# Mixer's division: a reciprocal-root seed on ScalarE and a third-order step on VectorE and GpSimd in place of VectorE's reciprocal, with the stages around it reordered

## The reference, cut to what matters

```python
h = layernorm(x) * (1 + ca) + sa
r  = sigmoid(h @ W_r.T + b_r)
ek = exp(h @ W_k.T + b_k)
v  = h @ W_v.T + b_v
td, g = exp(b_td), exp(global_decay)
# over the 1024 steps of each sequence:
sa  = ek_t * v_t + td * sa
sb  = ek_t + td * sb
wkv = (g * ek_t * v_t + sa) / (g * ek_t + sb + 1e-6)
mem = 0.3 * mem + r_t * wkv - 0.05 * (mem > 0.05)
spk = mem > 0.05
# then
x = x + ga * spk
```

## Time and profile before

| | us |
|---|---|
| median of 3 runs | 558.91 (558.04 to 559.72) |
| profiled execution, first to last instruction (span) | 556.3 |
| busy: PE 488.8, VectorE 432.2, ScalarE 348.2, GpSimd 334.6 | |
| mixer up to the first membrane instruction | 0 to 46.55 |
| membrane passes | 46.55 to 81.9 |
| norm and first tiles of attention | 81.9 to 112 |
| steady attention, MLPs, LRU, experts | 112 to 556.3 |

### The profile page before, as it was taken

The page is one execution under the profiler, slowest core; times in us unless marked ns, Lnnn a source line. Parts: engine busy times, 40 slices in busy tenths (PEclk is TensorE's granted clock), DMA queues, the critical chain, the costliest instruction groups (busy, mean ns, idle before and its releaser), DMA issues.

```text
span 556.3 us, 11701 instructions
## 1 busy us (share of the span) xinstructions
PE 488.8 (88%) x4017; PEld 307.6 (55%) x4017; DVE 432.2 (78%) x1172; ACT 348.2 (63%) x1002; POOL 334.6 (60%) x259
## 2 busy tenths in 40 slices
PE   5650048999999999999989999999999999999997
PEld 3320014467777777543457777777644445667775
DVE  6999999889999886556899999985545688366665
ACT  4971004689999997532579999998647526533332
POOL 5860006999999997776889999995010277420000
PEclk9885559999999999999989999999999999999999
DMA  8400002311111112000041111111000000000000
GB/s 290 165 0 1 1 1 78 69 37 41 39 37 33 39 41 86 2 1 0 2 113 41 40 35 35 41 39 39 1 3 0 0 1 1 1 0 20 20 20 20
DMA packets 14880, 19.93 MB, mean 36 GB/s; under 512 B 2362, under 2 KB 8996, under 8 KB 14692
## 3 DMA queue, kind: packets, MB, share of 16 engines
q1 hardware_dynamic: 14532, 19.08, 12.7%
q10 hardware_dynamic: 288, 0.08, 0.1%
HBM read 8.94 MB, written 1.05 MB: 18 GB/s over the span
## 4 chain that ended last, share of the span: by engine, by line
PE 68%; DVE 14%; POOL 6%; ACT 6%; issue 4%; DMA 1%; DVEq 0%; POOLq 0%; ACTq 0%
PE psT L1396 11%; PE psQK L1469 9%; PE psO L1591 6%; PE psO L1523 5%; PE psQK L1798 5%; PE psS L1571 5%; DVE vst L990 3%; DVE vAB L994 3%; PE psO L1396 3%; PE psS L1870 3%; PE psQK L1605 3%; PE psS L1707 3%; PE psO L1870 2%; PE psQK L1730 2%; PE psO L1709 2%
## 5 line engine op out<-in xcount | busy, mean ns | idle before, releaser
L526 ACT ACTIVATE prob<-psS,nmx 128x128 f32<-128x128 f32 x256 | 89.9, 377 | 18.0 <-DVE nmx L1135 18.0
L819 POOL TENSOR_TENSOR rn<-ssq,half 128x16 f32<-128x16 f32 x32 | 93.0, 2907 | 8.0 <-DVE ssq L1121 7.9
L811 POOL TENSOR_TENSOR ra<-ra,rb 128x512 f32<-128x512 f32 x64 | 80.9, 1284 | 1.0 <-DVE rb L1103 0.9
L666 POOL TENSOR_TENSOR rst<-mv,half 128x4 f32<-128x4 f32 x24 | 25.7, 1070 | 73.8 <-DVE mv L922 63.6
L1469 PE MATMUL psQK<-wqkv,hsA 128*128 128x512 f32 x128 | 62.0, 604 | 1.0 <-DVE hsA L1084 0.6
L526 ACT ACTIVATION_READ_ACCUMULATOR prob<-psS,nmx 128x1 f32 x256 | 55.6, 217 | 0.0
L1100 DVE TENSOR_TENSOR ra<-psQK,rope 128x512 f32<-128x512 f32 x64 | 43.9, 686 | 10.2 <-PE psQK L1469 9.7
L827 POOL TENSOR_TENSOR qkn<-ra,rn 128x512 f32<-128x512 f32 x32 | 49.0, 1532 | 2.5
L1103 DVE TENSOR_TENSOR rb<-psQK,rope 128x512 f32<-128x512 f32 x64 | 43.6, 681 | 0.0
L647 ACT ACTIVATE gel<-psQK 128x512 f32<-128x512 f32 x32 | 19.1, 597 | 37.5 <-PE psQK L1798 37.5
L1114 DVE TENSOR_REDUCE ssq<-sq 128x8 f32<-128x512 f32 x64 | 41.1, 677 | 1.6 <-ACT sq L466 1.3
(11 more groups left out here) (240 smaller groups left out, 1204.1 us busy)
## 6 DMA issues: line engine op xcount, KB each, us to landing
vAB<-vAB SPq DMA_DIRECT2D x62, 128.0 KB, 2.2
wqkv<-in_wqkv SPq DMA_DIRECT2D x2, 768.0 KB, 8.4
big<-in_x SPq DMA_DIRECT2D x4, 256.0 KB, 4.5
ropeb<-in_rope SPq DMA_DIRECT2D x1, 1024.0 KB, 6.5
big<-in_ew SPq DMA_DIRECT2D x2, 512.0 KB, 4.7
wmod<-in_wmod SPq DMA_DIRECT2D x2, 384.0 KB, 6.0
out<-big SPq DMA_DIRECT2D x3, 256.0 KB, 2.3
w<-in_w SPq DMA_DIRECT2D x2, 341.0 KB
```

Source lines behind the costliest of these rows:

```text
L526: act.activation(prob[:, k, :], psS[:, hb, c * P:(c + 1) * P], ACT.Exp, bias=nmx[:, k:k + 1], accum_out=sums[:, n % 2, k:k + 1]).then_inc( ...
L811: pool.tensor_tensor(o, o, rb[:, r], ALU.add).then_inc(s["sum_" + name], 1)
L819: pool.tensor_tensor(rn[:, :], ssq[:, :], half[:, :], ALU.pow).then_inc(s["rn_ready"], 1)
```

## The change

The division becomes: seed s = (1/sqrt(|d|))^2 by two activations on ScalarE, t = d*s, w = n*s, and quotient = w * ((t - 3)*t + 3). GpSimd makes w for all groups and t for groups 0 to 2; VectorE makes t for group 3 and the two remaining steps for all. The seeds are written over sb, for groups 0 and 1 once the second group's sb is there, so the division of all four groups follows all four numerators. The factor 20 moves from r to W_v and b_v (GpSimd), and ScalarE's four scalings go. Norms 2 and 3 go from ScalarE to GpSimd, in `mixer_norm`, with a semaphore of their own (`norms_done` chooses between the two). The transposes of x and their copies go behind the receptances and gates; r shares memory with ek, and has four banks. GpSimd's rope tables, the edges' memsets and the powers for the LRU go behind the currents, and VectorE makes the currents of groups 2 and 3.

The core of the diff:

```diff
@@ ScalarE
+            def division_seed(g):
+                last = (bof(g) + 1) * GPB
+                act.wait_ge(s["den_ready"], g + 1)
+                act.wait_ge(s["sb_ready"], last)
+                own.one(act.activation(sbb[:, gsl(g)], gek[:, gsl(g)], ACT.Abs_reciprocal_sqrt))
+                act.activation(sbb[:, gsl(g)], sbb[:, gsl(g)], ACT.Square).then_inc(s["seed_ready"], 1)
+            def receptance_gate(g):
+                act.wait_ge(s["r_mm"], g + 1)
+                act.wait_ge(s["sb_ready"], g + 1)
+                act.wait_ge(s["ekv_ready"], g + 1)
+                act.activation(rsg[:, gsl(g)], r_bank(g), ACT.Sigmoid, bias=vec[:, V_BR:V_BR + 1]).then_inc(s["r_ready"], 1)
             mixer_norm(0)
-            mixer_x(0)
             mixer_out(0)
+            mixer_norm(1)
             for g in range(NG):
...
-                if g == 0:
-                    mixer_norm(1)
                 if g + 1 < NG:
-                    mixer_x(g + 1)
                     mixer_out(g + 1)
-                if g + 2 < NG:
-                    mixer_norm(g + 2)
+            act.activation(sc[:, 11:12], half[:, 0:1], ACT.Abs_reciprocal_sqrt).then_inc(s["seed_table"], 1)
             for g in range(NG):
-                act.wait_ge(s["r_mm"], g + 1)
-                own.one(act.activation(rsg[:, gsl(g)], psQK[:, g % 2, :], ACT.Sigmoid, bias=vec[:, V_BR:V_BR + 1]))
-                act.activation(rsg[:, gsl(g)], rsg[:, gsl(g)], ACT.Copy, scale=20.0).then_inc(s["r_ready"], 1)
+                division_seed(g)
+            for g in range(NG):
+                receptance_gate(g)
+            for g in range(NG):
+                mixer_x(g)
@@ GpSimd
+            pool.wait_ge(s["ld_wr"], 16)
+            pool.tensor_scalar(wrkv[:, 2, :], wrkv[:, 2, :], SPIKES, 0.0, ALU.mult, ALU.add).then_inc(s["wv_ready"], 1)
...
+            for g in POOL_NORMS:
+                mixer_norm(g)
...
+            def weighed(g):
+                c = gsl(g)
+                pool.wait_ge(s["seed_ready"], g + 1)
+                pool.wait_ge(s["num_ready"], (bof(g) + 1) * GPB)
+                if g < NG - 1:
+                    pool.tensor_tensor(sab[:, c], gek[:, c], sbb[:, c], ALU.mult).then_inc(s["t_ready"], 1)
+                pool.tensor_tensor(ekv[:, c], ekv[:, c], sbb[:, c], ALU.mult).then_inc(s["w_ready"], 1)
@@ VectorE
-                dve.wait_ge(s["den_ready"], g + 1)
-                dve.reciprocal(gek[:, c], gek[:, c]).then_inc(s["rcp_ready"], 1)
+            def divided(g):
+                c = gsl(g)
+                if g == NG - 1:
+                    dve.wait_ge(s["seed_ready"], NG)
+                    own.one(dve.tensor_tensor(sab[:, c], gek[:, c], sbb[:, c], ALU.mult))
+                else:
+                    dve.wait_ge(s["t_ready"], g + 1)
+                own.one(dve.scalar_tensor_tensor(out=sab[:, c], in0=sab[:, c], scalar=-3.0, in1=sab[:, c],
+                                                 op0=ALU.add, op1=ALU.mult))
+                dve.wait_ge(s["w_ready"], g + 1)
+                dve.scalar_tensor_tensor(out=ekv[:, c], in0=sab[:, c], scalar=3.0, in1=ekv[:, c],
+                                         op0=ALU.add, op1=ALU.mult).then_inc(s["quot_ready"], 1)
+            for g in range(NG):
+                divided(g)
@@ PE
-            mixer_turn(0)
             ln_t2(ln_no(0, 0))
...
-                    mixer_turn(g + 1)
                     ln_t2(ln_no(0, g + 1))
             for g in range(NG):
                 receptance(g)
+            for g in range(NG):
+                mixer_turn(g)
```

More of the change, by code:

```diff
@@ L32 @@
 SEQ = 16
+POOL_NORMS = (2, 3)
+POOL_CURRENTS = 2
+SPIKES = 20.0
 NCH = T // SEQ
@@ L123, in program @@
         tvec = big[:, 5, 0:T]
-        ek, gek, ekv, sab, sbb, _, rsg = (big[:, i, :] for i in range(7))
+        ek, gek, ekv, sab, sbb = (big[:, i, :] for i in range(5))
+        rsg = ek
         oT = big[:, 0:4, :]
@@ L682, in rope_tables, with mixer_norm @@
                     i.then_inc(s["rope_ready"], 1)
+            def mixer_norm(g):
+                n = ln_no(0, g)
+                ln_rstd(n)
+                pool.wait_ge(s["ln_rstd"], n + 1)
+                pool.wait_ge(s["ln_t2"], n - 1)
+                for k in range(TPG):
+                    pool.tensor_scalar(lnx[:, n % 2, k, :], xt[:, g * TPG + k, :], rst[:, n, k:k + 1], nmr[:, n, k:k + 1],
+                                       ALU.mult, ALU.add).then_inc(s["own_norm"], 1)
             ln_rstd(ln_no(0, 0))
@@ L688, in _ @@
             pool.wait_ge(s["ld_c"], 16)
+            own.did(pool.tensor_scalar(sc[:, 10:11], vec[:, V_BV:V_BV + 1], SPIKES, 0.0, ALU.mult, ALU.add))
             own.one(pool.memset(fr[:, 0:1], float(np.e)))
@@ L717, in _ @@
                 pool.tensor_tensor(gek[:, gsl(g)], gek[:, gsl(g)], sbb[:, gsl(g)], ALU.add).then_inc(s["den_ready"], 1)
-                if g == 0:
-                    pool.wait_ge(s["ld_wa"], 64)
-                    rope_tables(0)
-                if g == 1:
-                    quotient(0)
-                elif g == 2:
-                    quotient(1)
-                    current(0)
-                    current(1)
-                    quotient(2)
-            current(2)
+            for g in range(NG):
+                weighed(g)
+            for g in range(POOL_CURRENTS):
+                current(g)
+            pool.wait_ge(s["w_ready"], NG)
+            pool.wait_ge(s["cur_ready"], POOL_CURRENTS)
+            pool.wait_ge(s["quot_ready"], NG)
+            pool.wait_ge(s["r_ready"], NG)
+            for k, edge in enumerate((hsA[64:128, T:T + 1], hsA[64:128, 0:1], hsM[64:128, T:T + 1], hsM[64:128, 0:1])):
+                pool.memset(edge, 0.0).then_inc(s["edges"], 1)
+                pool.wait_ge(s["edges"], k + 1)
+            pool.wait_ge(s["ld_wa"], 64)
+            rope_tables(0)
+            for dst, src in ((4, V_NU), (5, V_TH), (6, V_GAM)):
+                own.did(pool.tensor_tensor(sc[:, dst:dst + 1], fr[:, 0:1], vec[:, src:src + 1], ALU.pow))
+            own.sync()
+            own.one(pool.tensor_scalar(fr[:, 2:3], sc[:, 4:5], -1.0, 0.0, ALU.mult, ALU.add))
+            own.one(pool.tensor_tensor(sc[:, 7:8], fr[:, 0:1], fr[:, 2:3], ALU.pow))
             C1 = 1.0 / (2 * np.pi)
@@ L782, in phase_cosine @@
                 ts(wcs[:, 1, :], wlru[:, 3, :], c(11), 0.0, ALU.mult, ALU.add)
[L784 to L788 removed]
             def add_spikes(g):
                 pool.wait_ge(s["x_mixed"], g)
+                pool.wait_ge(s["xT_evac"], g + 1)
                 if g == 3:
@@ L961, in _ @@
                 dve.wait_ge(s["ek_ready"], g + 1)
-                dve.scalar_tensor_tensor(out=ekvp, in0=ekvp, scalar=vec[:, V_BV:V_BV + 1],
+                if g == 0:
+                    dve.wait_ge(s["sc_ready"], 1)
+                dve.scalar_tensor_tensor(out=ekvp, in0=ekvp, scalar=sc[:, 10:11],
                                          in1=ek[:, c], op0=ALU.add, op1=ALU.mult).then_inc(s["ekv_ready"], 1)
```

59 lines of the change are left out of this document (27 added, 32 removed).

## The result

The changed kernel is **slower**: 563.28 us median (562.82 to 564.25, 4 runs) against 559.32 for the kernel before beside it (558.04 to 559.85, 4 runs), a ratio of 1.0089 with the 95% interval 1.0072 to 1.0106. (The ratios here are estimates of their own and not the quotients of the two medians; that would be 1.0071 here.) The profiled execution of the changed kernel has a span of 561.0 us, 4.7 more than the 556.3 of before. A second set of four runs of the same kernel gave 563.31 us and 1.0098 [1.0079, 1.0118], its passes again from 48.29 to 87.66, as was expected of it.

A forecast was written before the change was run, and what follows sets the result against it. VectorE's membrane passes were taken to bound the kernel: starting 3.35 us later plus 4.5 us of rope tables gives 7.85, hence 566.7 us. Own range 565 to 569; wide range 561.5 to 570.5.

The forecast's parts named there:

- rival 1: Membrane passes: the late rope tables don't hold them up, since short instructions come first; shift 3.35 us, 562.3 us, chance 0.14.
- What bounds the kernel: VectorE's four membrane passes, 46.50 to 81.90 us: any later start or stretch of them moves the kernel's end by as much.
- Front half: Group loop before the division: 4.39 us a group, last g*ek ends at 28.7 instead of 32.56, GpSimd's norms cost nothing.
- Seeds: ScalarE's activations after the loop: a seed each 1.5 us, at 31.7, 33.2, 34.7 and 36.2, no gap around table loads.
- Division: After the numerators: GpSimd and VectorE exclude each other, so their work sums to 15.9 us, from 31.8 to 47.7.
- two currents: VectorE, between division and passes: 1.03 us each, with hand-overs putting the passes' start at 49.9, 3.35 later than 46.55.
- Rope tables: Four GpSimd products now beside VectorE's last currents and first membrane pass: hold up small instructions, cost 4 x 1.13 = 4.5 us.
- rival 2: Division: scalar_tensor_tensor steps don't exclude GpSimd, so the passes start 3.2 us earlier; 555.7 us, chance 0.08.
- rival 3: Front-half loop: TensorE's matmul pairs run at 1.2 GHz, 2.2 to 3 us more, up to 569.7; chance 0.07.
- rival 4: After pass 4: the division is too inexact, so the check triggers a fifth pass; 577 us or so, chance 0.02.

## Why the prediction came out

The mechanism came out, and the direction; the number did so less well. 563.28 us lies below the forecast's own range of 565 to 569 and inside the wide one only because that takes in two rivals. It is nearer to rival 1's 562.3 than to 566.7, so the time alone would have spoken for rival 1, whose mechanism the trace refutes (below). All four terms of the sum that are measured below were too long, none too short.

**What bounds the kernel.** Right. The start of the passes and their stretch went through: the closing comparison moved by 87.66 - 81.94 = 5.72 us, and layer 0 of the attention lies later by 5.7 to 5.8 all along.

**Front half.** Right in its order, 1 us too long. The last g*ek ended at 28.05, not 28.7, the first t product began at 30.83, not 31.8. I had added durations of ScalarE and hand-overs; exp and scaling, 0.69 and 0.72 long, do take 1.48 from 30.27 to 31.75, but g*ek overlaps with the output behind it: 14.73 + 0.81 is 15.54, and the output starts at 15.45. A loop is 4.17 and not 4.39. I had also let GpSimd wait for the last numerator; it didn't have to. Its first product needs the first seed (ready at 30.75) and its own last denominator (done at 30.80), and began 0.5 us before that numerator ended, at 31.34. GpSimd's norms cost nothing here, as said.

**Seeds.** An activation of this function takes 0.61 and the square 0.63, a seed 1.2 us and not 1.5. Only the first one could matter, and it came with the last denominator. The load at 28.07 follows the last g*ek at once and is followed at once, so this trace too shows no gap around a load.

**Division.** Right: 15.5 us from 30.83 to 46.32 against 15.9. The pace of a pair, one GpSimd product and one VectorE step, is 1.67 us and not 1.73. The two currents took 1.96 to the first membrane instruction and not 2.2. Start of the passes: 3.35 - 0.97 - 0.41 - 0.24 = 1.73 later, at 48.28 instead of 49.9.

**Rope tables.** Right in kind, 4.0 us instead of 4.5 (39.38 - 35.39). The first table began beside the second current, which it didn't delay, and so it held up the passes for 0.9 us only. Rival 1 fell with the pair of 2.52 us; rival 2 with the steps of 1.64 to 1.76; the pairs of 1.13 at 16.26, 20.43 and 24.60 ruled out rival 3 for this execution; the closing comparison came once, after four passes, so there was no fifth (rival 4).

One argument for this term was weaker than it read. The 128x4 instruction of 1.16 us at 89.73 stood for the small membrane instructions, but it is a tensor_scalar that reads one SBUF operand, and they read two. The membrane instructions did turn out to be held up; that row belongs to an exception, which the next section shows.

**What the sum left out.** 5.72 us at the passes' end, 4.7 in the span. The 0.95 between them came back at one place, the start of layer 1, and PE's rows show it: transposes that lie 5.69 us later at 281 us lie 4.76 later at 297, and the last ones of the kernel 4.74. The stretch (columns as in the earlier trace rows) and PE's transposes in it, of the kernel before:

```profile
281.00:283.00 2.00, 2.00 (x9) 1.89 (x10) 1.93 (x4) 1.62 (x7) 1.85 (x2) 0.55 0.85 184
```

```profile
280.96 1.80 PE L1396 MATMUL psT<-ident,qkn 128*128 128x128 f32 x8 [1.88 <-DVE qkn L1129]
```

The same of the changed kernel:

```profile
286.60:288.60 2.00, 1.95 (x11) 1.19 (x11) 1.93 (x4) 1.62 (x8) 1.86 (x2) 1.00 0.86 204
```

```profile
286.65 1.09 PE L1455 MATMUL psT<-ident,qkn 128*128 128x128 f32 x8 [1.88 <-DVE qkn L1188]
```

After the same gap of 1.88 us PE came back at a granted clock of 0.55 (1.2 GHz) before and 1.00 (2.4 GHz) after. Of the other profiled runs seven had it like the changed kernel, and the run of VectorE alone, the one with memsets and the one with the norms back did not. No edit of this change touches that place, so I count it as chance in the clock of an execution, not as a gain of the change. That is argued and not shown, and how often an execution gets it wasn't measured.

So the predicted 566.7 us was 3.4 too high, of which 1.6 are in the three terms 0.97 (front half), 0.41 (division) and 0.24 (currents), 0.5 in the tables and 0.95 in layer 1, which is chance by the above and here made the miss larger; the remaining 0.3 is the distance between a median and one execution.

## What to carry to other kernels

Before work is moved to GpSimd to relieve VectorE, count the SBUF operands of what VectorE does meanwhile: with two of them the engines take turns (a step of 0.69 became 1.7) and the help is negative; with one in SBUF and the other in PSUM, both ran at full speed, and that was worth 3.2 us here for the one operand that eight products share. The size of VectorE's instruction is no protection, a 128x64 step waits for a whole 128x512 table. And work that was free beside one instruction (a reciprocal) isn't free elsewhere: look up what stands at the new place at that time, in that kernel.

The count of operands is not the whole rule. The reciprocal reads one SBUF operand and loses nothing, but two other kinds of VectorE instruction with one SBUF operand were held up where they met GpSimd: the tensor_scalar of 128x4 (1.16 us at 89.73 against 0.17) and a copy of 64x512, here in the kernel before:

```profile
223.45 2.36 POOL L738 TENSOR_TENSOR big<-big,tsin 128x1024 f32<-128x1024 f32 x1
...
225.14 0.95 DVE L1082 COPY big<-z 64x512 f32<-64x512 f32 x1
```

Such a copy takes 0.42 us alone; this one ended at 226.09, 0.28 us after GpSimd's product. Yet another, at 217.86, took 0.43 in the middle of a GpSimd tensor_scalar of 3.65. So the rule above is shown for tensor_tensor, scalar_tensor_tensor, the scans and the reciprocal only; what sets copies and tensor_scalars apart, no run here tests.

## What the runs showed of the hardware

- Turns are a little cheaper than a plain sum: alone GpSimd's products start 1.22 us apart and VectorE's steps 0.60, together a pair takes 1.67, not 1.82.
- A scan with a broadcast first operand counts as a reader of two SBUF operands: 1.28 us became 2.35 beside rope tables.
- TensorE ran matmul pairs at 2.07 us, the rate of its lower level, in stretches whose granted clock reads 1.00: in the run with the early tables the pair at 16.66, behind transposes that took 1.06. The changed kernel ran the same transposes, 0.02 us earlier, in 0.61, and the pair in 1.13; three other runs had the slow transposes and then a fast pair (1.12 or 1.13). Two profiled runs of ten with the new order had this slow second pair, at 1.5 us each. The run with the norms back had a slow fourth (2.08), but there the granted clock reads 0.50. What decides it stays open; a profile of one execution can carry it, so differences under 1.5 us in the front half were read from the rows and not from the span.
